# Constant matrices prepared beside an earlier linear layer, their first products moved ahead of the first gathers, and the second step of a cell loop in another order

## The reference

```python
# layer 1, its end
h = relu(batchnorm(agg @ W1.T + b1, g1, be1))
out = batchnorm(h @ W2.T + b2, g2, be2)            # "second linear" below
# layer 2
h = relu(einsum('ts,bsh->bth', adj, x @ Wg0 + bg0))
h = relu(einsum('ts,bsh->bth', adj, h @ Wg1 + bg1))
for p in 1..4:                                      # LSTM over windows of p nodes, last state written back
    last = lstm_last(Wih[p-1], Whh[p-1], bih[p-1], bhh[p-1], windows(h, p))
    h[:, p-1::p] = last
# layer 3
h = x @ fc_in_w.T + fc_in_b
alph = sigmoid(alpha_train); w_eff = w * clip(d, 0, 1) @ w.T; dt = 1/8
for _ in range(8):
    h = h + dt * (alph*0.5*(adj @ h - h) + h @ w_eff - h + x0)
```

## Time and profile before

| | us |
|---|---|
| three runs | 982.57, 984.10, 989.01 |
| median | 984.1 |
| profiled execution, device time | 986.26 |
| its span | 984.10 |
| busy in the span: PE, DVE, ACT, POOL | 922.5, 652.3, 577.3, 303.8 |

### The profile page before, as it was taken

One profiled execution on the slowest core, in us unless ns is written; L12 is line 12 of the kernel. 1 busy time (PEld: TensorE's weight loads), 2 busy tenths in 40 slices (PEclk: granted clock), 3 DMA queues, 4 the chain that ended last, 5 costly groups with the idle time before them and its releaser, 6 DMA issues.

```text
span 984.1 us, 15023 instructions
## 1 busy us (share of the span) xinstructions
PE 922.5 (94%) x5121; PEld 798.1 (81%) x5121; DVE 652.3 (66%) x1586; ACT 577.3 (59%) x1290; POOL 303.8 (31%) x521
## 2 busy tenths in 40 slices
PE   8799999967999789999999999999999999988996
PEld 6688886456888468988998998899899889978986
DVE  6789994766477746666667657666765766664654
ACT  5466756743464537457647845764784586465452
POOL 3766551032210421044216204322621441230120
PEclk9999999988899889999999999999999999988999
DMA  5322101310001010101200110120001001000100
GB/s 176 120 74 65 65 33 55 138 65 0 33 1 55 1 33 1 54 1 44 65 1 12 44 55 1 44 65 1 27 29 54 2 22 44 1 11 1 33 22 22
DMA packets 26595, 38.55 MB, mean 39 GB/s; under 512 B 3333, under 2 KB 12422, under 8 KB 26010
## 3 DMA queue, kind: packets, MB, share of 16 engines
q1 hardware_dynamic: 26088, 36.05, 10.9%
q10 hardware_dynamic: 434, 1.57, 0.5%
HBM read 21.89 MB, written 15.73 MB: 38 GB/s over the span
## 4 chain that ended last, share of the span: by engine, by line
PE 55%; DVE 9%; POOL 7%; ACT 5%; issue 2%; ACTq 0%; POOLq 0%; DVEq 0%
PE psum L136 16%; PE psum L138 15%; PE psum L137 15%; PE psum L1787 2%; PE psum L1788 2%; PE psum L1791 2%; POOL out_rstd L1224 1%; POOL x_rstd L1224 1%; ACT x L1323 1%; ACT raw L1388 1%; ACT gate L1292 1%; DVE tl L1545 1%; POOL node_l L1242 1%; DVE x_stats L1481 1%; DVE nat_l L1659 1%
## 5 line engine op out<-in xcount | busy, mean ns | idle before, releaser
L1292 ACT ACTIVATE gate<-psum,gate_bias 128x256 f32<-128x256 f32 (+2 forms) x296 | 144.0, 559 | 85.4 <-PE psum L1791 71.9
L136 PE MATMUL psum<-in_h,wih_h 128*128 128x256 f32 (+2 forms) x312 | 108.0, 346 | 5.4 <-DVE in_l L1475 3.1
L137 PE MATMUL psum<-in_l,wih_h 128*128 128x256 f32 (+2 forms) x312 | 104.3, 334 | 0.0
L138 PE MATMUL psum<-in_h,wih_l 128*128 128x256 f32 (+2 forms) x312 | 104.1, 334 | 0.0
L1456 DVE TENSOR_TENSOR gate<-gate 128x256 f32<-128x256 f32 (+2 forms) x48 | 24.0, 499 | 94.7 <-ACT gate L1292 94.6
L136 PEld LDWEIGHTS psum<-in_h,wih_h 128*128 128x128 f32 x312 | 60.3, 193 | 16.7 <-DVE in_l L1475 6.2
L1258 POOL TENSOR_TENSOR gate<-in_h,in_l 128x512 f32<-128x512 f32 x14 | 17.9, 1307 | 167.4 <-DVE in_l L1475 167.4
L136 PE MATMUL psum<-e_h,th 128*128 128x384 f32 x180 | 62.9, 350 | 6.2 <-DVE tl L1545 5.3
L137 PEld LDWEIGHTS psum<-in_l,wih_h 128*128 128x128 f32 x312 | 60.2, 193 | 5.1 <-issue 0.2
L1295 ACT ACTIVATE gate<-cell 128x512 f32<-128x512 f32 (+2 forms) x80 | 40.3, 503 | 40.5 <-DVE cell L1459 35.2
L138 PEld LDWEIGHTS psum<-in_h,wih_l 128*128 128x128 f32 x312 | 60.0, 192 | 4.8
(11 more groups left out here) (397 smaller groups left out, 2957.2 us busy)
## 6 DMA issues: line engine op xcount, KB each, us to landing
x_spill<-x SPq DMA_DIRECT2D x30, 256.0 KB, 2.0
xt<-in_x_t_dram SPq DMA_DIRECT2D x16, 256.0 KB, 2.7
raw<-x_spill SPq DMA_DIRECT2D x16, 256.0 KB, 2.9
o_spill<-xt SPq DMA_DIRECT2D x14, 256.0 KB, 2.0
xt<-o_spill SPq DMA_DIRECT2D x14, 256.0 KB, 3.4
x<-x_spill SPq DMA_DIRECT2D x14, 256.0 KB, 3.7
out_dram<-raw SPq DMA_DIRECT2D x14, 256.0 KB, 2.3
raw<-in_adj_t_dram ACTq DMA_DIRECT2D x1, 1024.0 KB, 9.0
```

Source lines behind the costliest of these rows:

```text
L136: pe.matmul(dst, lh, rh, start=start, stop=False, **kw)
L137: pe.matmul(dst, lh, rl, start=False, stop=False, **kw)
L138: return pe.matmul(dst, ll, rh, start=False, stop=stop, **kw)
L1292: nc.scalar.activation(gate[q][:, 0:n], banks[GATE_BANK[q]][:, 0:n], ACT.Tanh if q == 2 else ACT.Sigmoid, bias=gate_bias[:, p - 1, q:q + 1 ...
```

## The change

**Into the second linear layer.** All preparations of M move there. The loops over batches are written out. POOL makes the two diagonals, `less_identity`, `scale_t` and the low halves of the transposed M; ACT gets, after relu of batch 2 and 3, a copy out of psum, after 4 to 7 a high half of M (`high_n`), after 9 to 12 a high half of its transpose (`high_t`); DVE gets `conv_bias` after batch 2, a low half of M (`low_n`) after 5 to 8, and `row_sum` after batch 12; PE gets the two broadcasts, before batch 0 and after batch 1. The sigmoid of alpha stands on ACT ahead of the loop. The results lie in one buffer `shared` whose four quarters held x1, xt and A_hat of layer 1 until then, and hold layer 3's `th`, `tl`, `x3h`, `x3l` later. `keep_busy` ahead of the loop falls from 18 to 12 times 4 quarter matmuls.

**START.** `first_0` and `first_1` stand ahead of the gathers, `first_2` between them; gathers and weights go in pairs. **Step 0.** After cell 1 come `square`, `twice`, `turn_0`, after cell 2 `first_3`; `mix_3` moves to step 1. **Step 1.** `lift` before `turn_0`; `x3t_0`, `power1` and `power2` of batch 0 all behind cell 3; `bias` behind cell 5, in another bank, and only the second tile of `coefs0_0` waits for it; low half of `e` on POOL. **Step 7.** `power1` and `power2` of batch 0 as in the steps before, `power2_1` whole behind cell 7.

```diff
-            keep_busy(18, 4)
+            keep_busy(12, 4)
...
+            def spread_column(v):
+                pe.wait_ge(cols_ready, v + 1)
+                for t in range(NT):
+                    mm = pe.matmul(tile(banks[2 + v][:], t), ones[:], diags[v][:, t, :], start=True, stop=True)
+                mm.then_inc(k_bc, 1)
+
+            pe.wait_ge(z_kept, HT * B)
+            spread_column(0)
+            for b in range(B):
+                second(b, b % 2)
+                if b == 1:
+                    spread_column(1)
...
+            for b in range(B):
+                relu(b, b % 2)
+                if 2 <= b < 4:
+                    keep_spread(3 - b)
+                if 4 <= b < 8:
+                    high_n(b - 4)
+                if 9 <= b < 13:
+                    high_t(b - 9)
...
+            def low_n(t):
+                dve.wait_ge(nat_hi, t + 1)
+                nc.vector.scalar_tensor_tensor(out=nat_l[:, t, :], in0=an[:, t, :], scalar=rates[:, t:t + 1], in1=f32(nat_h[:, t, :]),
+                                               op0=ALU.mult, op1=ALU.subtract)
+            for b in range(B):
+                keep_o2(b, b % 2)
+                if b == 2:
+                    dve.wait_ge(c_small, 16 * len(small))
+                    conv_bias_rows()
+                if 5 <= b < 9:
+                    low_n(b - 5)
+                if b == 12:
+                    row_sum()
...
-        START_PE = ["turn_0", "turn_1", "spread_0", "spread_1", "gather0_0", "weff", "weight0_0", "gather0_1", "gather1_0",
-                    "weight0_1", "weight1_0", "gather1_1", "first_0", "weight1_1"]
+        START_PE = ["turn_0", "turn_1", "weff", "first_0", "first_1", "gather0_0", "gather0_1", "weight0_0", "weight0_1", "first_2",
+                    "gather1_0", "gather1_1", "weight1_0", "weight1_1"]
...
+        START_ACT = ["prep_0", "prep_1", "first_0", "norm_0", "first_1", "norm_1", "gather0_0", "gather0_1", "weight0_0", "weight0_1",
+                     "first_2", "gather1_0", "gather1_1", "input_0", "input_1"]
...
-        ONCE_PE = [[], ["first_1", "first_2", "turn_0"], ["square", "first_3", "twice"], ["gather0_0", "cube", "second_0"],
+        ONCE_PE = [[], ["square", "twice", "turn_0"], ["first_3"], ["gather0_0", "cube", "second_0"],
...
-        NEXT_PE = [["hlate"], ["turn_0", "lift"], ["turn_vec", "x3t_0", "power1a_0"], ["power1b_0", "power2_0", "lift_last", "gather0_0"],
-                   ["bias", "weight0_0", "coefs0_0"]] + FILL_PE[5:]
+        NEXT_PE = [["hlate"], ["lift", "turn_0"], ["turn_vec"], ["x3t_0", "power1a_0", "power1b_0", "power2_0", "gather0_0"],
+                   ["lift_last", "weight0_0"], ["bias", "coefs0_0", "coefs1_0", "turn_1"]] + FILL_PE[6:]
+        NEXT_ACT = [[], ["evens_h"], ["x3norm_0", "x3split_0", "norm_0"], ["x3t_0", "evens_l", "power1_0", "power2_0", "gather0_0"],
+                    ["split_e", "rest_h", "prep_1", "weight0_0", "x3norm_1"], ["coefs0_0", "coefs1_0", "x3split_1", "rest_l"]] + FILL_ACT[6:]
...
-        LAST_PE = FILL_PE[:2] + [["x3t_0"], ["power1a_0", "power1b_0", "power2_0"], ["coefs0_0"], ["coefs1_0"],
-                                 ["x3t_1", "power1a_1", "power1b_1", "power2a_1"], ["power2b_1"], ["coefs0_1"], ["coefs1_1"],
-                                 ["inner_0", "inner_1", "hturn"]]
+        LAST_PE = FILL_PE[:8] + [["coefs0_1"], ["coefs1_1"], ["inner_0", "inner_1", "hturn"]]
```

More of the change, by code:

```diff
@@ L78, in program @@
         row_sums = sb("row_sums", [P, NT])
+        shared = sb("shared", [P, 4, NT, N], F32R)
+        rows_bc, conv_bias = sb("rows_bc", [P, N]), sb("conv_bias", [P, NT, D])
+        rates, vec = sb("rates", [P, NT]), sb("vec", [P, NT, 3])
+        steps = (shared, rows_bc, conv_bias, rates, vec)
         raw = sb("raw", [P, 2, NT, N])
@@ L284, in _ @@
             sp.dma_start(logits, adj_n).then_inc(c_an, 16)
-            with sp.Fori(0, B // 2 - 1) as i:
-                spill(2 * i, 0)
-                spill(2 * i + 1, 1)
+            for b in range(B - 2):
+                spill(b, b % 2)
             for par in range(2):
@@ new lines, in second_half @@
+        NEXT_ACT = [[], ["evens_h"], ["x3norm_0", "x3split_0", "norm_0"], ["x3t_0", "evens_l", "power1_0", "power2_0", "gather0_0"],
+                    ["split_e", "rest_h", "prep_1", "weight0_0", "x3norm_1"], ["coefs0_0", "coefs1_0", "x3split_1", "rest_l"]] + FILL_ACT[6:]
+        NEXT_DVE = [["addlate"], ["x3sum_0", "lift", "turn_0", "turn_vec"], ["mix_3", "x3sum_1", "mix_4"],
+                    ["x3t_0", "power1_0", "power2_0", "gather0_0", "mix_5", "mix_6", "mix_7"],
+                    ["lift_last", "weight0_0"], ["bias", "coefs0_0", "coefs1_0", "turn_1"]] + FILL_DVE[6:]
@@ L1930, in bflat @@
                 return bp[:, a:b, :].rearrange("p k d -> p (k d)")
-            def spread_column(v):
-                pe.wait_ge(cols_ready, v + 1)
-                for t in range(NT):
-                    mm = pe.matmul(tile(banks[v][:], t), ones2[:], diags[v][:, t, :], start=True, stop=True)
-                mm.then_inc(k_bc, 1)
             def weff():
@@ L2025, in bias @@
                 pe.wait_ge(vt_kept, 2)
[L2026 removed]
                 for t in range(NT):
[L2028 removed]
+                    mm = pe.matmul(tile(UB[1][:], t), tile(vec_t, t), bc, start=True, stop=True)
                 mm.then_inc(q_done, 1)
```

251 lines of the change are left out of this document (114 added, 137 removed).

## The result

The changed kernel takes 980.61 us (median of 11 runs, 979.04 to 981.96), the kernel before 987.64 (11 runs, 982.53 to 989.01); the ratio is 0.9941, with a 95% interval of 0.9922 to 0.9959. By the ratio that is 5.8 us faster, less than 1%, where 986 was forecast against 984.1, 2 us slower. The kernel before was timed anew with each group of kernels, and its median lay between 983.7 and 987.9, so kernels of different groups are compared by their ratios. The profiled execution took 981.68 us with a span of 979.6, against 986.26 and 984.1. The spans differ by 4.5 us, and the stages divide this as follows.

A forecast was written before the change was run, and what follows sets the result against it. PE, busy 94% of the span, was taken to bound the kernel. Second linear +6.3, START and step 0 -2.0, step 1 -1.0, step 7 -1.3 gave +2.0: 986 us against the median 984.1, range 973 to 995.

The forecast's parts named there:

- 8.7 plus half a microsecond of half clock around them: Step 1: gain from removing PE's waits of 2.98 and 5.70; against 8.2 of new waits it left -1.0 us.
- a wait of 2.50 is filled: Step 7: the wait ahead of power2 is filled by the rest of the same work, -1.3 us, bounds -2.5 and 0.
- Step 1's waits: Step 1: new waits for state 2.2, x's low half 1.2, power2_0 5.5 where 2.75 was, bias 3 for 0.9; sum 8.2.
- Second linear layer: Stage receiving the preparations: ACT's insertions and broadcasts +4.5, row_sum +0.8, conv_bias beside POOL +1.0; +6.3 us, bounds +1 and +10.6.
- low halves at 0.69 in the new place: Second linear layer: named sign that the forecast is wrong, DVE's low halves of M taking 0.69 us, against 1.77 in START.
- the two batches' buffers: Second linear layer: slack of two batches, which with 0.4 to spare cuts row_sum's 2.4 us block to about 0.8.
- the ring: Second linear layer: ACT's relu and PE's batches wait for each other, 1.78 us a batch, ACT having 0.26 to spare.
- START: START: products near 8 us, first gather 17.7 us in, tail chain about 3, stage 38.9 long; -2.65 us, -5 at full clock.
- Step 0: Step 0: PE idles 4.5 to 5 us ahead of twice; +0.65 us with twice at half clock, -2 at full.
- The first: Rival: the moves pay, with PE at full clock out of START; START and step 0 -7 to -9.6; 974 us, chance 0.17.
- The fourth: Rival: reorderings do nothing, each removed wait found again one piece later; steps 0, 1, 7 at zero; 988 us, chance 0.15.
- The third: Rival, second linear layer: two of four low halves meet POOL and pay 1.1 us each; 988 us, shares the forecast's chance.

The follow-up runs named there:

- both_lists: Kernel before with only the new PE lists of steps 1 and 7 (bias bank and low half of e included): 978.62 us, ratio 0.9920.
- start_only: Changed kernel with the lists of steps 1 and 7 taken back, leaving preparations, START and step 0 changed: 986.56 us, ratio 0.9996 to the kernel before.
- next_only: Kernel before with only the new lists of step 1, bias in the other bank and low half of e on POOL: 982.53 us, ratio 0.9973.
- prep_late: Changed kernel with row_sum and conv_bias moved from the second linear layer to DVE in START, behind weff: 976.18 us, ratio 0.9919.
- conv_late: Changed kernel with conv_bias alone moved to DVE in START, behind weff; row sum stays behind batch 12: 980.36 us, ratio 0.9955.
- start_fill: Changed kernel with nine and seven extra matmuls that nobody reads in PE's two waits of START: 979.82 us, ratio 0.9954.
- square_fill: prep_late with first_2 behind cell 1, square, first_3, twice behind cell 2 of step 0, plus start_fill's extra matmuls: 971.41 us, ratio 0.9878.
- combined: prep_late plus start_fill's extra matmuls, with first_2 and first_3 behind cell 1 of step 0, square and twice behind cell 2: 976.61 us, ratio 0.9923.

## Why the prediction was wrong

**Where it failed.** The sign was missed: +2.0 us forecast, -5.8 measured. `both_lists` and `start_only` divide the miss in two. The lists of steps 1 and 7 were put at -2.3 us; timed together they give -7.9 (-10.5 to -5.3), timed one by one -2.7 and -2.6. The preparations with START and step 0 were put at +4.3; timed, they give -0.4 (-2.4 to +1.7). So 3 to 5.6 us of the miss lie in the terms for steps 1 and 7, and about as much, 4.7, in the others. The forecast also held that a difference under 1% can hardly be told from none; the interval here is 0.4% wide.

In the first part the failing step is the sentence that the waits that go are worth "8.7 plus half a microsecond of half clock around them", and for step 7 that a wait of 2.50 is filled and nothing but waiting changes. The waits were summed, the clock was put at 0.5 us in step 1 and at none in step 7. The earlier trace rows had the sign of it: step 1 ran at 0.93 with 91.54 busy, and a step at full clock of 84.11 busy stood beside it. By an estimate from these rows the rise from 0.93 to 0.97 over 100 us is worth up to 4 us of PE's work; 1.7 to 1.8 of it show in step 1's busy time. In step 7 the 3.0 us of busy time (0.94 to 0.97 over 127 us) are those of one execution against one, and the kernel before had more half clock there than two others with its list; by timing the list gives 2.6, of which the waits are 1.1, so some 1.5 is left for the clock. The -1.3 of the waits themselves was right in size and wrong in its account: the wait of 2.50 was not filled, but the three waits of 0.70, 1.86 and 2.50 became two of 2.11 and 1.85 ahead of cells.

In the second part the terms that were mis-sized are the second linear layer (+6.3, measured +5.0) and START (-2.65, measured -4.5); what is wrong in each is said below.

**Step 1's waits** were right one by one: 2.2, up to 2.4 (1.2 taken), 5.5 and 3 were forecast, 1.97, 0.60, 5.60 and 2.36 measured. Net 1.8 less waiting, where the terms gave 0.5. In `next_only`, with nothing else changed, it is 1.2.

**Second linear layer.** +6.3 forecast, +5.0 in three kernels and +6.5 where the clock fell. The total came near, its parts did not: ACT's insertions and the broadcasts cost 2.2, not 4.5, and DVE's two blocks 2.8, not 1.8 (`prep_late`, `conv_late`). `conv_bias` beside POOL was forecast at 2.7 to 3.8 and took 3.04. The slow low halves of M did not come (0.73), as the sum had it: POOL was idle beside three of them and ended 0.16 us into the fourth. In `prep_late`, where POOL's own low halves began sooner beside them, the fourth on DVE took 1.17. So the sign "low halves at 0.69 in the new place" did come, without harm to the sum. The row sum costs 1.8 rather than 0.8. The term had allowed for "the two batches' buffers", and PE waited 1.56 for the statistics behind it (200.65); I take it that the ring gives no such allowance, which no run tests by itself.

**START.** -2.65 forecast, -4.5 measured. The first gather came 16.4 us in, not 17.7, as the clock rose within the first product (its twelve matmuls took 4.4, not 5.1 us), and the tail chain cost 1.8 (0.70 and 1.07 waited), not 3.

**Step 0.** +0.65 forecast, +0.8 measured, with the wait of 4.77 for the reason given and `twice` at 6.99 for 6.8.

**The half that I called costly.** Its terms as measured sum to +2.8 (6.5 - 4.5 + 0.8) or +1.3 with the 5.0; timed alone it is 0.4 us faster, between -2.4 and +1.7. The 1.3 lies within. I forecast +4.3 (6.3 - 2.0).

**The rivals.** The first, faster by full clock, was right in part of its mechanism but expected it in START and step 0 above all, at 974. START did rise from 0.79 to 0.91, step 0 fell from 0.96 to 0.92, and steps 1 and 7 rose to 0.97. The fourth, that each wait is found again one piece later, holds for most of the waiting in steps 1 and 7 (12.33 to 10.52, 5.06 to 3.96), and is still no reason for no gain. The third's two slow low halves did not come: the four took 0.73 each, and only the last overlapped with POOL, by 0.16 us.

What was not settled: the 1.0 us by which the first half was longer in the changed kernel's profile. Its lengths up to the first relu are 165.2 to 167.6 in all kernels, old and new, so I take it for scatter.

## What to carry to other kernels

Where PE bounds a kernel and the windows show a granted clock under 1, a wait can cost its own length and a part of the work behind it: price a removed wait by both, and a stage by its busy time against that of the same work at full clock. One profile of each kernel does not measure the second part, as step 7 showed; it takes timings of many executions, or profiles of several kernels that share the stage. Before a preparation is moved into a stage that looks free, write down who in it runs a ring without slack; on an engine inside the ring every inserted block counts, while the same block is free where its engine waits for a long product anyway. When two small steps depend on each other through another engine, put independent work between them, not ahead of both.

## What the runs showed of the hardware

The same wait of 1.86 to 1.87 us on PE was followed by half clock (matmuls of 128x384 at 0.52) in one execution and by full clock (0.33) in another; a stage with unchanged code and the same waits, step 7 with the tail, took 130.70 us with 10.2 at half clock ahead of the tail, and 126.79 with none.

Matmuls that nobody reads, started as PE falls idle, went with a full clock in START in two kernels (`start_fill` and `square_fill`, 1.00 against 0.90 or 0.91 without them), not in a third (`combined`, 0.95). Seven that started 1.28 us late were themselves slow (3.35 us).

Four TENSOR_SCALAR of 128x128 on DVE, 0.9 us alone, took 3.04 us beside POOL's TENSOR_TENSOR of 128x512, while POOL's own stayed at 1.28 each. The Trainium skill ("SBUF — State Buffer", "SBUF: two separate sides") says that the pair of ports that the two share is locked for a whole instruction, by a DVE operation in a 2-port mode or with two SBUF inputs or by one of POOL. The two operations of 1.31 us that end with one of POOL's, and the 0.28 of the last behind POOL, agree.
